# Small LayerNorm work moved from GpSimd to ScalarE and VectorE in a gated cross-attention and expert kernel

## The reference

```python
def xattn(x, adj, W, b):            # x is ctx, adj the normalized x
    si = einsum('bnd,d->bn', x, W[0, :D]); sj = einsum('bnd,d->bn', x, W[0, D:])
    return 0.6 * sigmoid(si[:, :, None] + sj[:, None, :] + b[0]) + 0.4 * adj

def ffn(x, wg, W, b):               # x is the normalized result of the line above
    probs = softmax(x @ wg); idx = argmax(probs); gate = probs[idx]
    return gate * (W[idx] @ x + b[idx])          # per token: one expert of 8

x = x + tanh(g_xattn) * xattn(ctx, layernorm(x), W1, b1)
x = x + tanh(g_ffn) * ffn(layernorm(x), wg, W, b)
```

## Time and profile before

| what | us |
|---|---|
| median of three runs (614.61 to 615.63) | 615.59 |
| the profiled execution, its own time | 615.98 |
| its span, first to last instruction | 614.3 |
| PE busy, of the span | 506.9 (83%) |
| DVE busy | 404.8 (66%) |
| POOL busy | 361.5 (59%) |
| ACT busy | 293.0 (48%) |

### The profile page before, as it was taken

One profiled execution on the slowest core, in us unless ns is written; L12 is line 12 of the kernel. 1 busy time (PEld: TensorE's weight loads), 2 busy tenths in 40 slices (PEclk: granted clock), 3 DMA queues, 4 the chain that ended last, 5 costly groups with the idle time before them and its releaser, 6 DMA issues.

```text
span 614.3 us, 14917 instructions
## 1 busy us (share of the span) xinstructions
PE 506.9 (83%) x2889; PEld 416.4 (68%) x2890; DVE 404.8 (66%) x529; ACT 293.0 (48%) x426; POOL 361.5 (59%) x537
## 2 busy tenths in 40 slices
PE   4676676666404999999999999999999999989980
PEld 4565565545303887887888888788888888878860
DVE  1777557785786777777777577778657857764230
ACT  2486556754312455455544454555445534553330
POOL 2596878889611364565555645655556465556662
PEclk9598778887755999999999999999999999999995
DMA  6952776783788588787888688897759777885520
GB/s 229 359 203 95 251 246 237 220 308 131 268 275 225 165 253 218 240 261 227 244 250 238 191 224 240 241 252 238 233 150 273 219 224 200 238 235 164 192 100 8
DMA packets 87751, 134.63 MB, mean 219 GB/s; under 512 B 11696, under 2 KB 69552, under 8 KB 87728
## 3 DMA queue, kind: packets, MB, share of 16 engines
q1 hardware_dynamic: 72464, 80.28, 46.6%
q0 software_dynamic: 15264, 54.06, 24.9%
HBM read 100.49 MB, written 35.91 MB: 222 GB/s over the span
## 4 chain that ended last, share of the span: by engine, by line
PE 21%; issue 19%; POOL 17%; DVE 16%; ACT 12%; ACTq 7%; DMA 2%; POOLq 2%; DVEq 1%; SPq 1%
PE pair L1151 13%; DVE xt L876 5%; DVE pair L884 5%; ACT rb L699 4%; ACT xt L691 4%; POOL scal L525 3%; POOL scal L528 3%; POOL table L490 2%; PE pair L1075 2%; PE pair L1066 2%; ACTq L732 2%; DVE xr L808 2%; DMA gates<-in_L_xattn_b 1%; ACT th L633 1%; POOL out_x L569 1%
## 5 line engine op out<-in xcount | busy, mean ns | idle before, releaser
L1151 PE MATMUL pair<-wt,xt 128*128 x1728 | 398.9, 393 | 31.8 <-DVE xt L876 27.3
L1151 PEld LDWEIGHTS pair<-wt,xt 128*128 128x128 f32 x1728 | 326.1, 189 | 104.3 <-issue 33.6
L536 POOL TENSOR_TENSOR rows<-rows,rb 128x1024 f32<-128x1024 f32 x37 | 89.5, 2420 | 2.9 <-ACT rb L713 1.6
L876 DVE TENSOR_TENSOR xt<-pair,xt 128x1024 f32 (+1 forms) x38 | 46.5, 1224 | 66.0 <-ACT xt L691 66.0
L685 ACT ACTIVATE wt<-pair 128x1024 f32 x56 | 57.6, 1028 | 55.9 <-DVE pair L884 51.7
L713 ACT ACTIVATE rb<-bias_bc,scal 128x1024 f32 (+1 forms) x37 | 46.0, 1244 | 71.1 <-POOL scal L532 71.1
L891 DVE TENSOR_TENSOR wt<-pair,wt 128x1024 f32 x56 | 67.9, 1212 | 13.0 <-ACT wt L685 13.0
L884 DVE STREAM_TRANSPOSE pair<-w_raw 128x1024 f32<-128x1024 f32 x56 | 69.4, 1239 | 1.0
L1075 PE MATMUL pair<-ident,xr 128*128 128x128 f32 x256 | 43.3, 324 | 31.6 <-DVE xr L808 31.5
L1075 PEld LDWEIGHTS pair<-ident,xr 128*128 128x128 f32 x256 | 35.9, 171 | 38.1 <-DVE xr L808 32.3
L295 POOL DMA_DIRECT2D rows<-table x38 | 23.2, 610 | 57.6 <-issue 27.0
(11 more groups left out here) (138 smaller groups left out, 407.5 us busy)
## 6 DMA issues: line engine op xcount, KB each, us to landing
w_raw<-in_L_ffn_W SPq DMA_DIRECT2D x264, 128.0 KB, 3.0
xb<-table SPq DMA_DIRECT2D x156, 128.0 KB
rows<-table POOLq DMA_DIRECT2D x38, 520.0 KB, 5.0
xr<-in_x SPq DMA_DIRECT2D x32, 512.0 KB, 6.3
ctx_in<-in_ctx SPq DMA_DIRECT2D x8, 512.0 KB, 5.3
bias_bc<-in_L_ffn_b SPq DMA_DIRECT2D x8, 512.0 KB, 6.2
out_x<-rows,scatter_row POOLq DMA_INDIRECT x36, 3.7
table<-xr,pos POOLq DMA_INDIRECT x32, 5.7
```

The costliest lines, as they stand in the source:

```text
L536: nc.gpsimd.tensor_tensor(rows[:, k, 0:H], rows[:, k, 0:H], rb[:, :], ALU.add).then_inc(base_ready, 1)
L876: nc.vector.tensor_tensor(xt[:, at, 1, :, :].rearrange("p a k n -> p (a k n)"), ps[:, :], xt[:, at, 0, :, :].rearrange("p a k n -> p (a k ...
L1151: last = nc.tensor.matmul(out_ps[r % 2][:, HALF * h:HALF * (h + 1)], xt[:, r % RING, x_part, k, :], wt[:, bass.ds(par, 1), w_part, k, HALF ...
```

## The change

1. POOL no longer makes `ln_a`, `ln_ma` and `ln_b`. It keeps the row numbers, variance plus epsilon and the power (`row_numbers`), now at the first tile of a group instead of the third.
2. DVE makes `ln_a` and the negative of `ln_ma` for four tiles at once (`norm_scalars`), behind the sum of the second tile of a group.
3. ACT makes `ln_b` (`shift`), one instruction of 128x1 per tile, behind the tanh of the tile after.
4. DVE takes moments up to tile t + 8 after the sum of tile t, at most two tiles at a time.
5. ACT issues the weights column and the three gate numbers; SP no longer does. ACT copies the first two contexts before it waits for the gates.
6. `ctx_sums` has two homes; for the first two groups PE sums both before it spreads either.

In the order of the listing: POOL, ACT, DVE, PE.

```diff
-            def norm_scalars(g):
+            def row_numbers(g):
...
-                link(nc.gpsimd.tensor_tensor(ln_r[:, four], ln_v[:, four], minus_half[:, :], ALU.pow))
-                link(nc.gpsimd.tensor_scalar(ln_a[:, four], ln_r[:, four], c_ln[:, 0:1], 1.0, ALU.mult, ALU.add))
-                link(nc.gpsimd.tensor_tensor(ln_ma[:, four], of_group(g, MEAN), ln_a[:, four], ALU.mult))
+                nc.gpsimd.tensor_tensor(ln_r[:, four], ln_v[:, four], minus_half[:, :],
+                                        ALU.pow).then_inc(root_ready, 1)
             def linear(t):
                 s = slot_of(t)
-                pool.wait_ge(th_ready, t + 1)
-                link(nc.gpsimd.tensor_scalar(ln_b[:, t:t + 1], xr[:, s, TH:TH + 1], nc2h[:, 0:1], ln_ma[:, t:t + 1],
-                                             ALU.mult, ALU.subtract))
+                pool.wait_ge(scales_of_tile, t // GR + 1)
+                pool.wait_ge(shift_ready, t + 1)
...
-                if r == 2 and g + 1 < NG:
-                    norm_scalars(g + 1)
+                if r == 0 and g + 1 < NG:
+                    row_numbers(g + 1)
...
-            act.wait_ge(gates_landed, 48)
-            nc.scalar.activation(th2[:, :], gates[:, 0:2], ACT.Tanh).then_inc(tanh_ready, 1)
+                act.dma_start(wcol[:, :], mix_w.rearrange("a (c p) -> p (a c)", p=P)).then_inc(wcol_landed, 16)
+            act.dma_start(gates[:, 0:1], g_xattn.unsqueeze(0).to_broadcast([P, 1])).then_inc(gates_landed, 16)
...
+            def shift(t):
+                act.wait_ge(th_ready, t + 1)
+                act.wait_ge(scales_of_tile, t // GR + 1)
+                nc.scalar.activation(ln_b[:, t:t + 1], xr[:, slot_of(t), TH:TH + 1], ACT.Identity,
+                                     scale=nc2h[:, 0:1], bias=ln_ma[:, t:t + 1]).then_inc(shift_ready, 1)
...
                 if r == 1 and g > 0:
                     logits_copy(g - 1)
+                if t + RTH - 2 < T:
+                    shift(t + RTH - 2)
                 copy_turned(t)
...
+            def norm_scalars(g):
+                four = slice(GR * g, GR * (g + 1))
+                dve.wait_ge(root_ready, g + 1)
+                link(nc.vector.tensor_scalar(ln_a[:, four], ln_r[:, four], c_ln[:, 0:1], 1.0, ALU.mult, ALU.add))
+                nc.vector.scalar_tensor_tensor(out=ln_ma[:, four], in0=of_group(g, MEAN), scalar=-1.0,
+                                               in1=ln_a[:, four], op0=ALU.mult, op1=ALU.mult).then_inc(scales_of_tile, 1)
...
+                if t == GR:
+                    norm_scalars(0)
+            seen = LEAD
             for t in range(T):
                 g, r = t // GR, t % GR
                 add_tanh(t)
+                if r == 1 and g + 1 < NG:
+                    norm_scalars(g + 1)
                 if r == 2 and g > 0:
                     position(g - 1)
-                if t + LEAD < T:
-                    stats(t + LEAD)
-                    moments(t + LEAD)
+                for n in range(2):
+                    if seen < T and seen <= t + LEAD + 2:
+                        stats(seen)
+                        moments(seen)
+                        seen += 1
...
             for g in range(2):
                 sum_context(g)
+            for g in range(2):
                 spread_context(g)
```

More of the change, by code:

```diff
@@ L149, in build @@
             wg_sb = sb("wg_sb", [P, K, CG], where=zone)
-            ctx_sums = sb("ctx_sums", [P, P], where=zone)
+            ctx_sums = sb("ctx_sums", [P, 2, P], where=zone)
             row_j = sb("row_j", [P, GR, P], where=zone)
@@ L214, in build @@
         lin_ready = sem("lin_ready")
+        root_ready = sem("root_ready")
+        scales_of_tile = sem("scales_of_tile")
+        shift_ready = sem("shift_ready")
         xc_ready = sem("xc_ready")
@@ L270, in slot_of, with of_group @@
             return t % RX
+        def of_group(g, col):
+            s = slot_of(GR * g)
+            return xr[:, s:s + GR, col:col + 1].rearrange("p r a -> p (r a)")
         def tile_of(rows_of, t):
@@ L315, in _ @@
                 load_context(g)
[L316 to L320, removed]
             for t in range(4):
@@ L493, in store @@
                     bounds_check=E * N - 1, oob_is_err=False).then_inc(row_stored[s], 16)
-            norm_scalars(0)
+            row_numbers(0)
             linear(0)
@@ L598, in settled @@
                 act.sem_inc(act_passed, 1)
-            act.wait_ge(gates_landed, 48)
-            nc.scalar.activation(th2[:, :], gates[:, 0:2], ACT.Tanh).then_inc(tanh_ready, 1)
+            with nc.allow_non_contiguous_dma(reason="512 weights, once, as columns"):
+                act.dma_start(wcol[:, :], mix_w.rearrange("a (c p) -> p (a c)", p=P)).then_inc(wcol_landed, 16)
+            act.dma_start(gates[:, 0:1], g_xattn.unsqueeze(0).to_broadcast([P, 1])).then_inc(gates_landed, 16)
+            act.dma_start(gates[:, 1:2], g_ffn.unsqueeze(0).to_broadcast([P, 1])).then_inc(gates_landed, 16)
+            act.dma_start(gates[:, 2:3], mix_b.unsqueeze(0).to_broadcast([P, 1])).then_inc(gates_landed, 16)
             def context_copy(g):
@@ L611, in context_sums @@
                 act.wait_ge(ctx_summed, g + 1)
-                if g:
-                    act.wait_ge(spread, g)
-                nc.scalar.activation(ctx_sums[:, :], ctx_sum(g), ACT.Identity,
+                if g > 1:
+                    act.wait_ge(spread, g - 1)
+                nc.scalar.activation(ctx_sums[:, g % 2, :], ctx_sum(g), ACT.Identity,
                                      bias=quarter_b[:, 0:1]).then_inc(sums_ready, 1)
@@ L654, in _ @@
                 context_sums(g)
+            act.wait_ge(gates_landed, 48)
+            nc.scalar.activation(th2[:, :], gates[:, 0:2], ACT.Tanh).then_inc(tanh_ready, 1)
+            for g in range(2):
                 context_spread(g)
+            act.wait_ge(scales_ready, 1)
             for t in range(RTH - 1):
                 half_tanh(t)
+                if t:
+                    shift(t - 1)
             for t in range(T):
@@ L1065, in spread_context @@
                 for c in range(GR):
-                    nc.tensor.matmul(sj_sum(g)[:, c, :], row_j[:, c, :], ctx_sums[:, :], start=True, stop=True)
-                nc.tensor.matmul(si_sum(g), ctx_sums[:, :], ident[:, :].rearrange("p (c r) -> p r c", r=CG)[:, 0, :],
+                    nc.tensor.matmul(sj_sum(g)[:, c, :], row_j[:, c, :], ctx_sums[:, g % 2, :], start=True, stop=True)
+                nc.tensor.matmul(si_sum(g), ctx_sums[:, g % 2, :], ident[:, :].rearrange("p (c r) -> p r c", r=CG)[:, 0, :],
                                  start=True, stop=True).then_inc(spread, 1)
```

## The result

| what | before | after |
|---|---|---|
| median of three runs, us | 615.59 | 641.34 (641.27 to 644.79) |
| ratio, with its 95% interval | | 1.0427 [1.0388, 1.0465] |
| profiled execution: own time, span, us | 615.98, 614.3 | 641.34, 639.7 |

The account below looks back on a forecast made before the run. The prediction took VectorE's hand-ordered queue and its round trips to set routing's pace, with a fixed expert stage after. +21.0 for four groups, -2.6 for GpSimd, 0 for the start, on 615.98, gave about 634 us, range 621 to 645.

Parts of the forecast that it names:

- The deciding step: VectorE's moments two tiles earlier in routing: tiles 16, 20, 24, 28 wait for their slots, +21.0 us over four groups.
- first store behind the choice: GpSimd's store of a group's first tile goes out 9.6 us after the choice, against 7.7 before.
- tile to next choice: Moments, sum, slow transpose, logits and hand-overs from the tile's landing to the next choice: 6.0 us, 5.1 at the low end.
- The trip: Store out of a slot plus load into it: 8.6 and 7.1 us in the trace, mean 7.85 taken.
- The shift's price: ScalarE's shift of a tile, behind the next tile's tanh, was taken to last 0.25 us.
- GpSimd's relief: Work shed by GpSimd shortens VectorE's waits in the tail: -2.6 us, between 0 and -5.2.
- The start: Earlier loads against scales and root waits before the first groups: 0 us, low end -2, high end +2.
- That routing passes to the end: A microsecond won or lost in routing is one of the whole, since the expert stage is fixed work afterwards.
- the relief: Rival: tile lateness vanishes in VectorE's logits waits, GpSimd waits go and the start wins 2: 608.8 us, chance 0.10.
- the nothing: Rival: the tile wait merely replaces each group's logits wait and the rest cancels: 616 us, chance 0.03.
- The small stall: Rival: the store follows the positions at once, four groups cost +8.6 us: 622 us, chance 0.12.
- The long trips: Rival: a group's stores and reloads slow each other, 2 us more per trip: 642 us and beyond, chance 0.05.

Follow-up runs that it names:

- lead six: The changed kernel with moments six tiles ahead instead of eight, row numbers and scales at a group's third tile: 618.79 us, ratio 1.0029.
- the lead alone: The kernel before with only the moments taken eight tiles ahead, scale and shift still on GpSimd: 631.96 us, ratio 1.0253.
- the scales: The kernel before with the front, and VectorE making each group's scales behind its third tile's sum: 613.75 us, ratio 0.9945.
- the front: The kernel before with ScalarE's small loads, contexts copied first, two homes for context sums and TensorE's new order: 614.97 us, ratio 0.9984.
- the second run: The kernel before with the front and the shift on ScalarE, sign turned, linear step as multiply and subtract: 685.20 us, ratio 1.109.

## Why the prediction was right, and which terms were mis-sized

*The deciding step* held: four waits for tiles 16, 20, 24 and 28, and choices 23.28 to 24.13 us apart where 23.4 was forecast. Four groups cost +22.5, forecast +21.0. Inside the cycle of choice 3 the errors cancel in part, which is luck:

| step | forecast | measured |
|---|---|---|
| first store behind the choice | 9.6 | 10.8 |
| store and load landed, VectorE goes on | 7.85 | 7.1 |
| tile to next choice | 6.0 | 6.2 |
| sum | 23.4 | 24.1 |

The store was later than forecast because the tanh in front of the shift was: `si_half` came 4.65 us behind the choice, before 4.02 (109.00 less 104.98), since TensorE's work ahead of the context's spread took longer, the gate multiplication and the sum of the context 1.08 us each (121.29 and 122.15 above). Before:

```profile
104.87 0.64 PE L1087 MATMUL pair<-xc_tr,wg_sb 128*32 128x128 f32 x16
...
105.33 0.87 PE L1058 MATMUL pair<-ctx_tr,wij 128*32 128x128 f32 x16
```

The rest is 0.13 for the shift and 0.27 for a linear step of 1.47. The trip, 3.4 and 3.6 us, was a little shorter than even the low end of the earlier trace rows, 7.1. The estimate of 6.4 us from the Trainium skill ("DMA: Bandwidth & Descriptors", "Anatomy of one DMA") lies 0.6 below these 7.0 us, my mean 0.85 above; both miss by about as much. The Trainium skill states it there for transfers that GpSimd issues, as the store is; the load is issued by SP.

*The shift's price* of 0.25 us was too small (0.38), and its place mattered beyond the store: the runs show 0.8 to 1.0% for it at lead six too, where the forecast had nothing. In the changed kernel VectorE waits for x in the four groups, and this comes out only as the later store.

*GpSimd's relief* was the step that failed: -2.6 forecast for the tail, +0.45 measured. VectorE's waits for GpSimd's linear step did fall, from 5.2 to 1.6, in the tail from 2.5 to 1.1. But in the tail it now waits 1.3 for GpSimd's root, which the forecast had only in the first groups, and 9.7 for logits and ranks where it waited 9.1. Together 12.1 us against 11.6, which is about the +0.45.

*The start* was taken at 0 and cost 1.46. The first sum came earlier, in part as the low end had it, but the sum of tile 3, which ends group 0, came 3.8 us later. Before:

```profile
25.48 1.28 DVE L808 SCALAR_TENSOR_TENSOR xr<-th,c,xr 128x1024 f32<-128x1024 f32 x1 [0.45 <-POOL xr L482]
...
33.55 1.28 DVE L808 SCALAR_TENSOR_TENSOR xr<-th,c,xr 128x1024 f32<-128x1024 f32 x1
```

The changed kernel:

```profile
24.33 1.28 DVE L827 SCALAR_TENSOR_TENSOR xr<-th,c,xr 128x1024 f32<-128x1024 f32 x1 [0.46 <-POOL xr L477]
...
30.85 0.23 DVE L820 TENSOR_SCALAR ln_a<-ln_r,c_ln 128x4 f32<-128x4 f32 x1 [1.26 <-POOL ln_r L470]
...
37.36 1.55 DVE L827 SCALAR_TENSOR_TENSOR xr<-th,c,xr 128x1024 f32<-128x1024 f32 x1
```

Between these sums VectorE now also waits 1.26 us for the root, which the text had in its high end, makes scales (1.1 us), and takes the moments of five tiles instead of three, which the text did not count. Which of these makes the 1.46 at choice 0 was not separated; with the lead alone on the kernel before, choice 0 comes at 48.67, no later than before.

*That routing passes to the end* held: 24.45 of the 25.4 us are there at choice 7.

Of the rivals, the relief and the nothing would have needed the tile in time, and it was not. The small stall supposed that the store follows the positions at once (C + 6.4); it went out at C + 10.8. The long trips did not come: they took 7.0. The sum forecast, 634, is 7 us low: 1.5 for the groups, 3.05 for the tail, 1.46 for the start and 0.95 behind choice 7 make 6.96. The small terms of tail and start both came out as costs; that 641.3 still lies inside the range, 3.7 us from its end, is owed to the width of the range and not to them.

## What to carry to other kernels

Where a ring of buffers feeds an in-order queue, compare when a buffer can be back (its last use, its store, its load) with when the queue asks for it, before asking earlier: here 5.7 us to spare in the group of tile 28 became a wait of 5.7. A small operation that is moved to a less busy engine also waits for what stands ahead of it in that engine's queue: here 0.38 us of work cost 0.8 to 1.0%. That the queue's order is the whole of this price is not shown, since moving it ahead of the tanh did not win it back. When a change of several parts loses, run the parts alone: here one of them, the scales, wins 0.55% together with the front.

## What was not expected of the hardware

- GpSimd's step over 128x1024 took 1.20 us as multiply and add (tile 5 above) and 4141 ns in the mean as multiply and subtract, on tiles of the same size with two scalars from memory; the second run is 10% longer by it.
- ScalarE's 128x1 instruction with scale and bias from memory takes 0.38 us, over twice its 128x4 copy (0.17).
- TensorE's transposes take 1.95 or 1.97 us all through the four groups, before 1.95 or 1.09: the granted clock of a group is 0.57 to 0.59, mostly the level of 1.2 GHz, and TensorE idles 3.8 to 5.1 us at a time in it, waiting for VectorE's sum. Here the stall on VectorE so also slows the engine that has to catch up.
- The gates landed later though they were issued earlier, by ScalarE in place of SP. In order of time, VectorE's first use:

```profile
13.38 0.15 DVE L798 TENSOR_SCALAR quarter_b<-gates 128x1 f32<-128x1 f32 x1 [7.62 <-DMA gates<-in_L_xattn_b]
```

The last gate was issued at 2.58, so 10.8 us passed; before, it was issued at 3.58 and used at 12.62, 9.0 us. Whether the queue does this or the loads of x on SP, which began two microseconds earlier (2.02 in place of 4.06), was not tried.
